# A gated, quantized layer with a per-sequence adapter: the down-projection two steps behind the up-projection instead of three, and the starting work in another order

## The reference, cut to what matters

```python
scale = cond @ norm_w.T + 1.0
h = x * (scale[:, None, :] * rsqrt(mean(x * x, -1) + 1e-6))
val, gate = split(h @ up_w.T, 2, axis=-1)             # 2 x 1024
h = val * gelu(gate, exact)
hq = round(h * s) clipped to +-128, over s            # s = 127 / max|h| of a row
wq = ternary(down_w)                                  # by the mean of |down_w|
x1 = hq @ wq.T + x                                    # down-projection and residual
Wd_b = Wd + 0.1 * (cond @ Wdd.T + bdd)                # 128 x 256 for each sequence
Wu_b = Wu + 0.1 * (cond @ Wdu.T + bdu)                # 256 x 128 for each sequence
out = x1 + relu(x1 @ Wd_b.T + bd) @ Wu_b.T + bu
```

## Time and profile before

| what | us |
|---|---|
| median of 3 runs (lowest, highest) | 527.75 (527.22, 527.75) |
| the profiled execution's own time | 527.7 |
| its span | 525.8 |
| TensorE busy with matmuls | 468.2 (89%) |
| VectorE busy | 380.9 (72%) |
| ScalarE busy | 363.7 (69%) |
| GpSimd busy | 237.7 (45%) |
| mean granted TensorE clock, of full speed | 0.987 |

### The profile page before, as it was taken

How to read it: one execution, slowest core, us unless ns; L and a number is a source line. 1 busy time by engine, 2 the same in 40 slices (tenths; PEclk the granted TensorE clock), 3 DMA queues, 4 the chain that set the end, 5 groups by cost and what they waited for, 6 DMA issues and landing times. The chain is left out here.

```text
span 525.8 us, 9822 instructions
## 1 busy us (share of the span) xinstructions
PE 468.2 (89%) x3206; PEld 260.5 (50%) x3206; DVE 380.9 (72%) x832; ACT 363.7 (69%) x632; POOL 237.7 (45%) x569
## 2 busy tenths in 40 slices
PE   2677999999999889999899999989999999999954
PEld 1234555555555445555455545555554555455432
DVE  3589888988888776767677776766677767667752
ACT  4579788898885677676766777676766666776541
POOL 0161556445562245455554445564444333333552
...
DMA packets 120402, 71.64 MB, mean 136 GB/s; under 512 B 104672, under 2 KB 105376, under 8 KB 118176
## 3 DMA queue, kind: packets, MB, share of 16 engines
...
## 5 line engine op out<-in xcount | busy, mean ns | idle before, releaser
L676 PE MATMUL bank<-up_hi,xs_hi 128*128 128x512 f16 x512 | 153.6, 382 | 11.1 <-DVE xs_lo L536 5.7
L414 ACT ACTIVATE gel<-bank,rms 128x512 f32<-128x512 f32 x128 | 87.0, 680 | 107.8 <-POOL rms L343 55.9
L676 PE MATMUL bank<-up_hi,xs_lo 128*128 128x512 f16 x512 | 153.2, 381 | 0.0
L676 PE MATMUL bank<-up_lo,xs_hi 128*128 128x512 f16 x512 | 153.2, 381 | 0.0
L557 DVE SCALAR_TENSOR_TENSOR hid<-bank,rms,gel 128x512 f32<-128x512 f32 x128 | 95.8, 748 | 42.5 <-ACT gel L414 41.3
L332 POOL TENSOR_TENSOR nwt<-nwt 128x2 f32<-128x2 f32 x96 | 28.1, 292 | 165.6 <-DVE nwt L550 160.5
L419 ACT ACTIVATE hid<-hid,amax 128x1024 f32<-128x1024 f32 x64 | 73.0, 1141 | 11.3 <-DVE amax L571 11.2
L676 PEld LDWEIGHTS bank<-up_lo,xs_hi 128*128 128x128 f16 x512 | 50.3, 98 | 61.4 <-issue 1.6
L676 PEld LDWEIGHTS bank<-up_hi,xs_lo 128*128 128x128 f16 x512 | 50.3, 98 | 61.0 <-issue 1.1
L565 DVE TENSOR_REDUCE amax<-hid 128x1 f32<-128x1024 f32 x64 | 78.1, 1220 | 2.2
L676 PEld LDWEIGHTS bank<-up_hi,xs_hi 128*128 128x128 f16 x512 | 48.9, 98 | 46.5 <-issue 8.2
...
## 6 DMA issues: line engine op xcount, KB each, us to landing
xT_s<-in_xT SPq DMA_DIRECT2D x32, 256.0 KB, 3.1
xn_s<-in_xn SPq DMA_DIRECT2D x32, 256.0 KB, 3.1
...
out<-out_s SPq DMA_DIRECT2D x32, 256.0 KB, 2.4
...
x<-in_down_wT SPq DMA_DIRECT2D x1, 1024.0 KB, 13.4
qT<-qn SPq DMA_TRANSPOSE x64, 3.1
```

The lines of the kernel that those rows point to most:

```text
L414: nc.scalar.activation(gel[:, c], u_gate[c][:], ACT.Gelu, scale=rms[:, t // TPB % XN_SLOTS, t % TPB:t % TPB + 1]).then_inc(gelu_done, 1)
L676: ins = nc.tensor.matmul(dst[:], a[:, t // TPB % 2, k, cols], w[:, c, k, v, :], start=(k == 0 and n == 0), stop=(k == KD - 1 and n == 2))
```

## The change

The same instructions are done, in another order, with these edits. DOWN goes from 3 to 2, and `qT` has two places instead of three. `out_s` has three places instead of two. `adapter_step` gives 2 b + 6 instead of 2 b + 7, so from sequence 20 on the middle stands in an even step, one earlier, and of the last three sequences the middle one moves from NT + 1 to NT + 2. Squares, guess and Newton steps of a sequence b stand in step 2 b - 2 (squares at the end of 2 b - 3) instead of 2 b - 1. The three loads for the condition are issued by ScalarE, ahead of SyncE's first load of up_w; the small loads are waited for at their first use. In ScalarE's step, the high part of the generators comes ahead of the squares. The sum of |down_w| is taken at the end of step 1, TensorE's sum and the ternary weights are in step 2. The base of the adapter weights is made in step 1. GpSimd takes 1152 of 2048 columns of a chunk from the first chunk on (768 in the first two before). In steps from NT on, `total` comes behind the low part, and a transpose of x1 is issued in its own step, behind that of qT.

The diff, without the hunks that only replace `pool_cols(q)` by the constant and without the body of `base_sum`'s waits in `evacuate`:

```diff
@@ -46,6 +46,8 @@
 NGEN = 2 * NGC
 GENERATED = 2 * NGEN
 
+POOL_COLS = 1152
+
 
 U_SCALE = 256.0
 W_SCALE = 256.0
@@ -54,18 +56,18 @@
 
 XT_SLOTS = 2
 XN_SLOTS = 4
-QT_SLOTS = 3
+QT_SLOTS = 2
 AM_SLOTS = 8
 X1_SLOTS = 20
 X1N_SLOTS = 4
 X1T_SLOTS = 3
 AD_SLOTS = 3
-OUT_SLOTS = 2
+OUT_SLOTS = 3
 N_SMALL = 6
 N_NEWTON = 11
 
 
-DOWN = 3
+DOWN = 2
 
 END = NT + 6
@@ -73,13 +75,18 @@
 def adapter_step(b):
 
     if b >= B - 3:
-        return (NT, NT + 1, NT + 3)[b - B + 3]
-    return max(2 * b + 7, NGEN + 3 + (4 * b + 2) // 3)
+        return (NT, NT + 2, NT + 3)[b - B + 3]
+    return max(2 * b + 6, NGEN + 3 + (4 * b + 2) // 3)
 
 
 ADAPT = [adapter_step(b) for b in range(B)]
 
 
+def scales(s):
+
+    return [b for b in range(1, B) if max(2 * b - 2, 1) == s]
+
+
 def sequences(s, lead):
 
     return [b for b in range(B) if ADAPT[b] - lead == s]
@@ -276,27 +278,28 @@
                 sp.wait_ge(out_done, b + 1)
                 sp.dma_start(out[b], out_s[:, b % OUT_SLOTS]).then_inc(stored[b % OUT_SLOTS], 16)
 
-            for half in range(2):
-                sp.dma_start(cond2[half * C:(half + 1) * C, :], condT).then_inc(ld_cond, 16)
-            sp.dma_start(normw[:], norm_wT).then_inc(ld_cond, 16)
             for n in range(NC * KD):
                 sp.dma_start(raw_up[:, n // KD, n % KD], up_wT[:, n // KD, n % KD]).then_inc(ld_up[n], 16)
                 if n == 0:
                     load_x(0)
             load_chunk(0)
+            load_x(1)
             for i, (w, b) in enumerate(((WdT, bddT), (WuT, bduT))):
                 sp.dma_start(base[:, i, :], w).then_inc(ld_small, 16)
                 sp.dma_start(bias_raw[:, i, :], b).then_inc(ld_small, 16)
             sp.dma_start(bd_col[:], bd).then_inc(ld_small, 16)
             sp.dma_start(bu_row[:], bu.to_broadcast([P, D])).then_inc(ld_small, 16)
-            load_x(1)
+            load_chunk(1)
             sp.dma_start(raw_down, down_wT).then_inc(ld_down, 16)
-            load_chunk(1)
             for s in range(END):
-                for t in split_tiles(s - 1):
-                    transpose_x1(t)
+                if s <= NT:
+                    for t in split_tiles(s - 1):
+                        transpose_x1(t)
                 if 0 <= s - 1 < NT:
                     transpose_q(s - 1)
+                if s >= NT:
+                    for t in split_tiles(s):
+                        transpose_x1(t)
                 for b in sequences(s, -2):
                     store(b)
                 if s % TPB == 0 and s // TPB + 2 < B:
@@ -306,7 +309,7 @@
 
             sp.wait_ge(turn, 2 * NT)
             for i in range(OUT_SLOTS):
-                sp.wait_ge(stored[i], 16 * (B // OUT_SLOTS))
+                sp.wait_ge(stored[i], 16 * len(range(i, B, OUT_SLOTS)))
 
         @block.gpsimd
         def _(pool):
@@ -351,6 +354,8 @@
                 ins.then_inc(ad_done, 1)
 
             def output_bias(b):
+                if b == 0:
+                    pool.wait_ge(ld_small, 16 * N_SMALL)
                 pool.wait_ge(x1_done, b * TPB + TPB)
                 after(pool, stored[b % OUT_SLOTS], 16 * (b // OUT_SLOTS))
                 for i in range(TPB):
@@ -362,12 +367,11 @@
                 nc.gpsimd.tensor_tensor(mid_lo[:], mid[:], mid_hi[:], ALU.subtract).then_inc(mid_done, 1)
 
             rsqrt(0)
-            pool.wait_ge(ld_small, 16 * N_SMALL)
             for s in range(END):
                 for b in sequences(s, -1):
                     middle_low(b)
-                if s % TPB == 1 and s // TPB + 1 < B:
-                    rsqrt(s // TPB + 1)
+                for b in scales(s):
+                    rsqrt(b)
                 for b in sequences(s, 2):
                     adapter_low(b)
                 for b in sequences(s, 0):
@@ -434,6 +438,8 @@
                 nc.scalar.copy(x1n[:, t % X1N_SLOTS, 0], x1[:, t % X1_SLOTS]).then_inc(x1_hi_done, 1)
 
             def relu(b):
+                if b == 0:
+                    act.wait_ge(ld_small, 16 * N_SMALL)
                 act.wait_ge(mid_full, b + 1)
                 after(act, mid_done, b)
                 after(act, o_full, b)
@@ -441,6 +447,9 @@
                     nc.scalar.activation(dst[:], mid_ps[:, 0:S], ACT.Relu, bias=bd_col[:, 0:1],
                                          scale=1.0 / A_SCALE).then_inc(relu_done, 1)
 
+            act.dma_start(normw[:], norm_wT).then_inc(ld_cond, 16)
+            for half in range(2):
+                act.dma_start(cond2[half * C:(half + 1) * C, :], condT).then_inc(ld_cond, 16)
             act.wait_ge(const_ready, 2)
             nc.scalar.activation(warm[:], zero[:], ACT.Gelu)
@@ -450,32 +459,35 @@
                                      ).then_inc(up_hi_ready, 1)
                 if n == 0:
                     scaled_high(0)
-            squares(0)
-            act.wait_ge(ld_small, 16 * N_SMALL)
+                if n == 1:
+                    squares(0)
             for s in range(END):
                 for b in sequences(s, -1):
                     relu(b)
                 if s < NT:
                     gelu(s, 0)
-                    if s > 0:
-                        quantize(s - 1)
-                for t in split_tiles(s):
-                    residual_high(t)
-                if s == NT:
+                if 0 <= s - 1 < NT:
                     quantize(s - 1)
+                if s < NT:
+                    for t in split_tiles(s):
+                        residual_high(t)
                 if 0 <= s - 1 < NT:
                     quantized(s - 1)
+                if s >= NT:
+                    for t in split_tiles(s):
+                        residual_high(t)
                 if s < NT:
                     gelu(s, 1)
                 if s % TPB == 0 and s // TPB + 1 < B:
                     scaled_high(s // TPB + 1)
-                    squares(s // TPB + 1)
-                if s == 0:
+                if s < NGEN:
+                    high_part(s)
+                for b in scales(s + 1):
+                    squares(b)
+                if s == 1:
                     act.wait_ge(ld_down, 16)
                     nc.scalar.activation(tern[:].rearrange("p j d -> p (j d)"), raw_down, ACT.Abs,
                                          accum_out=wsum[:, 0:1]).then_inc(absum_ready, 1)
-                if s < NGEN:
-                    high_part(s)
 
         @block.vector
         def _(dve):
@@ -513,6 +527,13 @@
                     scalar=DELTA_SCALE * A_SCALE / (W_SCALE * C_SCALE),
                     in1=base[:, w, at:at + 2 * BCH].unsqueeze(2).to_broadcast([P, 2 * BCH, B]),
                     op0=ALU.mult, op1=ALU.add).then_inc(gen_done, 1)
+
+            def base_sum():
+                dve.wait_ge(ld_small, 16 * N_SMALL)
+                nc.vector.scalar_tensor_tensor(out=base[:], in0=bias_raw[:], scalar=DELTA_SCALE, in1=base[:],
+                                               op0=ALU.mult, op1=ALU.add).then_inc(base_ready, 1)
+                dve.wait_ge(base_ready, 1)
+                nc.vector.tensor_scalar(base[:], base[:], A_SCALE, None, ALU.mult).then_inc(base_ready, 1)
 
             def ternary():
                 dve.wait_ge(absum_full, 1)
@@ -618,27 +639,24 @@
                 if n == 0:
                     scaled_low(0)
             rsqrt_guess(0)
-            dve.wait_ge(ld_small, 16 * N_SMALL)
-            nc.vector.scalar_tensor_tensor(out=base[:], in0=bias_raw[:], scalar=DELTA_SCALE, in1=base[:],
-                                           op0=ALU.mult, op1=ALU.add).then_inc(base_ready, 1)
-            dve.wait_ge(base_ready, 1)
-            nc.vector.tensor_scalar(base[:], base[:], A_SCALE, None, ALU.mult).then_inc(base_ready, 1)
-            dve.wait_ge(base_ready, 2)
             for s in range(END):
                 if s < NT:
                     gate(s, 0)
+                if s == 1:
+                    base_sum()
+                if s == 2:
+                    ternary()
                 if 0 <= s - DOWN < NT:
                     dequantization(s - DOWN)
                     residual(s - DOWN)
-                for b in sequences(s, -2):
-                    total(b)
+                if s < NT:
+                    for b in sequences(s, -2):
+                        total(b)
                 if 2 <= s < NGEN + 2:
                     evacuate(s - 2, 0)
                     evacuate(s - 2, 1)
-                if s % TPB == 1 and s // TPB + 1 < B:
-                    rsqrt_guess(s // TPB + 1)
-                if s == 1:
-                    ternary()
+                for b in scales(s):
+                    rsqrt_guess(b)
                 if s % TPB == 0 and s // TPB + 1 < B:
                     scaled_low(s // TPB + 1)
                 for b in sequences(s, 2):
```

10 lines of the change are left out of this document (5 added, 5 removed).

## The result

The changed kernel takes 558.15 us (median of 4 runs, 554.82 to 560.51); the kernel before took 527.62 beside it. The ratio is 1.0576, 95% interval 1.052 to 1.0631. The forecast was 537.4 us, with a range that ended at 543: the sign was right, the size was off by a factor of three.

The account below looks back on a forecast made before the run. TensorE was taken to bound the generation steps, later nearly matched by a loop through ScalarE and VectorE that the change lengthens. Start +4.0, middle -4.0, late +10.8, tail -1.1 gave +9.7 on 527.7: 537.4 us, range 526 to 543.

Parts of the forecast that it names:

- Generation steps: Steps 5 to 16: TensorE bounds them and the operand lands in time; 0 us, bounds 0 and +3.
- Late steps: Steps 44 to 62: the operand's loop makes two steps take 15.4 us against 14.2; +10.8 us.
- the sum: Late even steps: second gate 6.44, reciprocal 2.22, transpose issue 3.36, landing 3.1; 15.1 us, the least for two steps.
- Steps 16 to 44: Middle steps: without the rms wait four steps take 29.2 us where they took 29.8; -4.0 us, bounds 0 and -10.
- -10 bound: Steps 16 to 44: the gain if TensorE never waits, 28.1 us per four steps.
- The start: Up to pos(5), the down-projection of step 5: earlier gelu, then waits for ternary rounding and half clock; +4.0 us.
- Tail: After the last steps: last down-projection one step earlier, last adapter unmoved; -1.1 us, bounds -3 and +2.
- 1: Late steps: operand in time, TensorE bounds, 13.4 us a pair, -7.2 in place of +10.8; 519.4 us, 13 in 100.
- 2: Late steps: TensorE waits for qT what it waited for mid_lo, pair stays at 14.2; 526.6 us, 7 in 100.
- 3: VectorE and GpSimd block fully, pair takes 15.8 us, more waits in generation steps; 541 to 544 us, 15 in 100.

Follow-up runs that it names:

- e4: The changed kernel with the next chunk's load issued behind the transposition of q instead of ahead of it; 547.64 us, ratio 1.0383.
- h2: The kernel before with the down-projection two steps behind, two qT places and the chunk's load behind the transposition of q; 532.78 us, ratio 1.0117.
- e8: The changed kernel with the next chunk's load on ScalarE's queue, issued earlier in the step; 563.39 us, ratio 1.072.
- e6: The changed kernel with the chunk's load behind the transposition of q and GpSimd's low part started after VectorE's; 538.86 us, ratio 1.0244.
- f5: The changed kernel with the down-projection three steps behind again and GpSimd's low part started after VectorE's; 508.71 us, ratio 0.9692.
- e1: The changed kernel with the down-projection three steps behind again and three places for qT, all other moves kept; 516.37 us, ratio 0.9784.
- e5: The changed kernel with VectorE's casts of the adapters' high parts ahead of the guess and of xs_lo; 551.12 us, ratio 1.0495.
- e2: The kernel before with the down-projection two steps behind and two places for qT, nothing else; 552.43 us, ratio 1.047.
- e7: The changed kernel with the adapters' steps as in the kernel before; 542.8 us, ratio 1.0346.
- f7: The changed kernel with the down-projection three steps behind, GpSimd's low part after VectorE's and the adapters' steps as before; 503.38 us, ratio 0.9592.
- h4: The kernel of f7 with the three small loads back at the head of SyncE's queue; 503.85 us, ratio 0.9572.

## Why the prediction was wrong, by its steps

**Generation steps, 0 with bounds 0 and +3: wrong, measured +12.3.** This is the largest error. Two sentences failed. "The operand landed 0.4 us or more before a place two steps behind" was worked with 3.1 us, the median landing of the whole run, while in these very steps of the kernel before it was 5.6 to 7.2 us. The load that causes it stands in the same queue, and the prediction never asked what SyncE issues just ahead of the transposition. e4 and h2, which only move the load, show that this is the cause. Whether the load delays the transposition by its place in the queue or by its bytes in flight stays open (e8). And "VectorE has more than that to spare" was not read from a row: behind the low part VectorE has the evacuation, and TensorE wants the buffer that it frees. The same edit, e6 against e4 and f5 against e1, shows 5.8 and 7.4 us for it. The meeting itself was forecast, with the right size (+1.9 against the 3.20 - 1.07 = 2.13 above).

**Late steps, +10.8 with two steps at 15.4: right, measured +11.7 with 15.50.** The chain of an even step, from pos(52) = 439.54:

```profile
445.99 0.75 DVE L578 SCALAR_TENSOR_TENSOR hid<-bank,rms,gel 128x512 f32<-128x512 f32 x1
447.41 1.41 POOL L362 TENSOR_TENSOR out_s<-x,bu_row 128x256 f32<-128x256 f32 x2
448.21 0.17 DVE L592 RECIPROCAL amax<-amax 128x1 f32<-128x1 f32 x1
448.30 0.80 DVE L614 TENSOR_TENSOR x1n<-x,x1n 128x256 f16<-128x256 f32 x1
450.49 0.40 ACT L438 CAST x1n<-x 128x256 f16<-128x256 f32 x1 [0.93 <-DVE x L607]
450.80 1.05 ACT L431 ACTIVATE qn<-hid 128x1024 bf16<-128x1024 f32 x1
451.97 1.23 SPq L267 DMA_TRANSPOSE qT<-qn  x1
```

The second gate is at +6.45 (forecast 6.44), the reciprocal 2.22 later (2.22), the issue 3.76 later (3.36), the landing 3.08 (3.1): 15.51 where the sum said 15.1, and 15.4 with the 0.3 us taken for residual_low. That one is visible too: 0.80 us beside GpSimd's output_bias (to 448.82), where it takes 0.41 without it. So the terms of the sum are right. What the prediction made of them is only partly so. It named adapter_high's new place as what costs, and by e5 that is a fifth. It took the operand to be 1.0 us late "with everything else as it is", and e2 has a late pair of 14.06 us for most: the 3.36 us in the sum hold a wait for x1 that a lead of two brings back only together with the shift (e7 and e2 issue after 2.70 and 2.72). And it did not see that the shift also costs at a lead of three (f7).

**Steps 16 to 44, -4.0: wrong, measured +1.5, outside the bounds** (0 and -10). Links from a step divisible by four were put at 14.5 us and took 14.45 to 14.81 (14.81 from pos(32)). The others were put at 14.7 and took 15.47 to 15.94 (15.47 from pos(30), 15.54 from pos(34), 15.94 from pos(42)): that is where most of the error lies. The link from pos(34):

```profile
306.89 1.35 DVE L557 SCALAR_TENSOR_TENSOR xs_lo<-xT_s,scaleT,xs_hi 128x256 f16<-128x256 f32 x2 [3.09 <-ACT xs_hi L401]
307.04 1.79 POOL L362 TENSOR_TENSOR out_s<-x,bu_row 128x256 f32<-128x256 f32 x2
310.97 2.51 SPq L274 DMA_TRANSPOSE x1T<-x1n  x2
312.24 1.05 ACT L431 ACTIVATE qn<-hid 128x1024 bf16<-128x1024 f32 x1
313.60 2.27 SPq L267 DMA_TRANSPOSE qT<-qn  x1
```

xs_lo takes 1.35 us where it takes 0.88 with GpSimd idle. The step has two tiles of x1, so two transpositions keep SyncE's queue to 313.48, while qn is ready at 313.29. Issue at +11.95 and landing 3.6 later: +15.5. "Without the rms wait their operand needs about 14.4" counted none of this. That the moves had a gain here is shown by e1: 195.3 us, 12.7 under the kernel before, with 28.15 us per four steps, which is the -10 bound's 28.1. The lead of two took all of it. These causes are read from the rows. Only the place of adapter_high was moved alone (e5), for 2.9 us; no run took away the others.

**The start, +4.0: direction right, +2.7.** Errors cancel in part. TensorE's first matmul waited 7.3 us for the small loads on their new queue, against 4.4 before, and h4, with the loads back, is the same as f7. Still, gelu 0 started at 18.45 (forecast 18.0, before 20.13) and the first down-projection at 39.05 (forecast 39.6). The clock cost less than the 3 us taken. Behind the first down-projection the rows are

```profile
39.05 1.25 PE L707 MATMUL bank<-tern,qT 128*128 128x256 bf16 x5 [5.39 <-DVE tern L551]
...
40.73 1.06 PE L697 MATMUL bank<-up_hi,xs_hi 128*128 128x512 f16 x2
41.59 1.06 PE L697 MATMUL bank<-up_lo,xs_hi 128*128 128x512 f16 x2
...
43.03 0.59 PE L697 MATMUL bank<-up_hi,xs_hi 128*128 128x512 f16 x2
```

1.06 us for a pair that takes 0.59 at 2.4 GHz: TensorE ran at 1.2 GHz from 39.05 to about 42.7, half of which, 1.8 us, is lost. The granted clock was 0.53 between 39 and 43 us and 1.00 between 43 and 47. Against that, pos(3) to pos(5) took 17.5 us and not two steps of 8.18, with 2.0 us of waits for VectorE's low part and evacuation, as in the generation steps.

**Tail, -1.1: right, -1.0.**

**The rivals.** 1 and 2 needed an operand in time and fell. 3, the lock in full and a few waits in the generation steps, named the right place with a quarter of the price. Nothing in the list of cases had the operand late behind a load, so the range ended 12 us below the fastest run.
